# Attention and FP4 feed-forward block: job order within a unit, a lead of 23 chunks, and value products two units behind their scores

## The chip, the cores and the metric

The kernel runs on one core of a Trainium2 chip. The metric is the device time of one execution in microseconds (us). The kernel before was run three times: 900.21, 903.68 and 904.95 us, median 903.68. A further execution was profiled; the trace rows below come from it.

## What is computed

The input x is 4 x 1024 tokens of width 128. It is normalized, and two branches are added to it:

```python
xn = _layernorm(x, axis=-1)
x = x + attn(xn, Wq, bq, Wk, bk, Wv, bv, Wo, bo) + ffn(xn, w_gate, w_up, w_down)
# attn: 16 heads of 8 columns
scores = jnp.einsum('bhqd,bhkd->bhqk', q, k) * scale + bias[None]   # alibi bias
attn = jax.nn.softmax(scores, axis=-1)
ctx = jnp.einsum('bhqk,bhkd->bhqd', attn, v)
# ffn: every operand of the three products is rounded to FP4 in blocks of 16
h = jax.nn.silu(fp4_linear(x, w_gate)) * fp4_linear(x, w_up)        # 352 columns
return fp4_linear(h, w_down)
```

## The kernel before, in words

Softmax needs the maximum of each row of scores. The kernel computes every score twice. In the first pass TensorE makes a **chunk**: 128 queries of one head against all 1024 keys, as two matmuls of 512 columns into one of two PSUM slots `mx` (`half_chunk`, L925 to L938). VectorE reduces the chunk to its negated maximum (L811). The maxima of 16 chunks (four heads, half of the queries) are split into two bf16 parts (L816, L817), transposed (`turn`, L944), copied by ScalarE (L636), and sent through DRAM into two rows of the operand `q_op` (`max_rows`, L379 and L382). In the second pass a score matmul therefore already has its maximum subtracted; it gives 128 keys x 512 queries of one head (`score`, L947 to L956), and ScalarE takes the exponential (L630) into `probs`. A value product (`value_product`, L958 to L969) multiplies the `probs` of four heads with v, as four matmuls beside each other in the columns of the array, in two passes, and accumulates over eight key tiles in the PSUM bank `pv`.

The work is cut in 256 **units** U: four heads, half of the queries, one key tile of 128. A unit holds four scores (j = 0 to 3), the value product of the unit before, and two chunks (i = 0, 1) of the first pass, which runs LEAD = 22 chunks ahead. Every eighth unit closes a `pv` bank: ScalarE copies it (L667), then the job `pvT` transposes and scales it. Score banks are a ring of three in `low`; a matmul into the ring waits until the entry three places before is emptied, and all entries of the ring are emptied by ScalarE. The two slots `mx` are a ring of their own, emptied by VectorE.

The order in TensorE's queue is written out by hand (L1067 to L1078). For i = 0, 1 and kh = 0, 1 it is half a chunk, then score j = 2i + kh. The jobs of the unit (`extras(U)`) come after i = 0, and value product U - 1 comes at the end. Which rows of the array an operand uses depends on its head: `head_rows(x, ...)` gives rows 0 up for x = 0 and rows 64 up for x = 1. A chunk has 51 rows, a score 53. These two lines set x:

```python
    x, g, qt = c % 2, c // 8, c // 2 % 4          # in chunk(pos); c = pos % 16, pos = LEAD + 2 * U + i
HEAD = ((1, 0), (1, 1), (0, 0), (0, 1))           # (x, g) of score j
```

Jobs, with the offset f of a unit in a feed-forward period of 15 units (16 periods, for 256 tokens each): `xT` 0, `gate` 1 and 2, `up` 4, `hT` 12 and 13, `down` 14; the quantization of the next period is spread over GpSimd and VectorE (`block_maxima` L784, `block_scales` L795 to L798, `powers` L804) between f = 5 and 12. For token groups 2 to 7 there are `xnT`, `q`, `k`, `v`, and at the end of a batch `ctxT` and `wo`. `up`, `down`, `pvT`, `wo` and `bvo` use an `mx` slot and are emptied by VectorE; the others use a bank of `low` and are emptied by ScalarE.

Of the kernel before, what the change touches and what calls it, by code (L numbers as in the profile page):

```python
# [23 lines left out]
KT = S // P  # L24
HALF = S // 2
UNITS = 2 * KT
NU = B * QUADS * UNITS
# [41 lines left out]

LEAD = 22
CHUNKS = 2 * B * QUADS * UNITS
HALVES = 2 * B * QUADS

# [1 line left out]
def ffn_unit(p):  # L77
    return 10 + 15 * p


def group_unit(g):
    return 13 + 60 * (g // 2 - 1) + 15 * (g % 2)


def turn_unit(m):
# [18 lines left out]
def extras(U):  # L104

    out = []
    p, f = divmod(U - ffn_unit(0), ffn_unit(1) - ffn_unit(0))
    if 0 <= p < NP:
        out += {0: [("xT", p)], 1: [("gate", p, 0)], 2: [("gate", p, 1)], 4: [("up", p)], 12: [("hT", p, 0)],
                13: [("hT", p, 1)], 14: [("down", p)]}.get(f, [])  # L110
    for g in range(2, NG):
        if 0 <= U - group_unit(g) < 4:
            out.append((("xnT", "q", "k", "v")[U - group_unit(g)], g))
    out += [("turn", m) for m in range(LEAD // 16, HALVES) if turn_unit(m) == U]
    m, f = U // KT - 1, U % KT
    if m >= 0:
        out += [("pvT", m)] * (f == 2)
        if m // 2 % QUADS == QUADS - 1:
            out += {4: [("ctxT", m // 8 * 2 + m % 2)], 5: [("wo", m // 8 * 2 + m % 2)]}.get(f, [])
    out += {0: [("bvo",)], 7: [("gT",)], 8: [("uT",)], 9: [("dT",)]}.get(U, [])  # L120
    return out


IN_DVE_RING = ("up", "down", "pvT", "wo", "bvo")


def rings():

    act, dve = {}, {}

    def to_act(*key):
        act[key] = len(act)

    def to_dve(*key):
        dve[key] = len(dve)

    for g in range(2):
        for name in ("xnT", "q", "k", "v"):
            to_act(name, g)
    for pos in range(LEAD):  # L140
        to_dve("max", pos)
        if pos == 17:
            to_act("turn", 0)
    for U in range(NU + KT):
        for i in range(2):
            if LEAD + 2 * U + i < CHUNKS:
                to_dve("max", LEAD + 2 * U + i)
            for j in (2 * i, 2 * i + 1):
                if U < NU:
                    to_act("exp", U, j)  # L150
            for job in extras(U) if i == 0 else ():
                (to_dve if job[0] in IN_DVE_RING else to_act)(*job)
    return act, dve


# [3 lines left out]
def attn_ffn(nc, x, wq, bq, wk, bk, wv, bv, wo, bo, wg, wu, wd, out):  # L159
    with ExitStack() as ctx:  # L160
# [260 lines left out]
        def _(pool):  # L421
# [136 lines left out]
            for U in range(NU):  # L558
                b, u = divmod(U, QUADS * UNITS)
                if u == 2:  # L560
                    add_bias(b)
                for g in range(2, NG):
                    if U == group_unit(g) - 2:
                        normalize(g)
                    if U == group_unit(g) + 2:
                        three_parts(g, 0, "q")
                    if U == group_unit(g) + 3:
                        three_parts(g, 1, "k")
                for p in range(NP):
                    if U == ffn_unit(p) + 3:  # L570
                        swish(p)
                    if U == ffn_unit(p) + 5:
                        scale_to_grid(p + 1)
                    if U == ffn_unit(p) + 7:
                        round_on_grid(p + 1)


# [1 line left out]
        def _(act):  # L579
# [77 lines left out]
            for U in range(NU + KT):  # L657
                if 3 <= U < NU:
                    act.wait_ge(pv_done, U - 2)
                for j in range(2):  # L660
                    exponential(U, j)
                if U % KT == 1 and U > KT:
                    m = U // KT - 1
                    act.wait_ge(pv_done, U - 1)
                    if m:
                        act.wait_ge(mx_full, MX["pvT", m - 1] + 1)
                    nc.scalar.copy(pv_s[:], pv).then_inc(pv_kept, 1)  # L667
                for job in extras(U):
                    kind, p = job[0], job[1] if len(job) > 1 else 0
                    if kind == "xT":  # L670
                        full("xT", p)
                        if p:
                            act.wait_ge(mx_full, MX["up", p - 1] + 1)
                        nc.scalar.copy(xqT[:], bank("xT", p)[:, 0:PW]).then_inc(st_free, 1)
                    elif kind == "gate":
                        t = job[2]
                        full("gate", p, t)
                        if p:
                            act.wait_ge(mx_free, MX["up", p - 1] + 1)
                        nc.scalar.activation(tanh_s[:, t * I:(t + 1) * I], bank("gate", p, t)[:, 0:I], ACT.Tanh, scale=0.5)  # L680
                        nc.scalar.copy(gate_s[:, t * I:(t + 1) * I], bank("gate", p, t)[:, 0:I]).then_inc(st_free, 1)  # L681
                    elif kind == "hT":
                        t = job[2]
                        full("hT", p, t)
                        if p:
                            act.wait_ge(mx_full, MX["down", p - 1] + 1)
                        nc.scalar.copy(hqT[t][:], bank("hT", p, t)[:, 0:3 * P]).then_inc(st_free, 1)
                    elif kind == "xnT":
                        keep_xnT(p)
                    elif kind == "q":  # L690
                        keep_q(p)
                    elif kind == "k":
                        keep_k(p)
                    elif kind == "v":
                        keep_v(p)
                    elif kind == "turn":
                        keep_turn(p)
                    elif kind == "ctxT":
                        full("ctxT", p)
                        if p:  # L700
                            act.wait_ge(mx_full, MX["wo", p - 1] + 1)
                        nc.scalar.copy(ctxT_s[:], bank("ctxT", p)).then_inc(st_free, 1)
                    elif kind in ("gT", "uT"):
                        full(kind)
                        nc.scalar.copy((gT_s if kind == "gT" else uT_s)[:], bank(kind)[:, 0:I]).then_inc(st_free, 1)
                    elif kind == "dT":
                        full("dT")
                        nc.scalar.copy(dT_s[:, 0:2 * P], bank("dT")[:, 0:2 * P])
                        nc.scalar.copy(dT_s[0:96, 2 * P:3 * P], bank("dT")[0:96, 2 * P:3 * P]).then_inc(st_free, 1)
                for j in range(2, 4):  # L710
                    exponential(U, j)


        @block.vector
        def _(dve):
# [74 lines left out]
            def block_scales(job):  # L790
                n = job_cols(job) // BLK
                settle()
                if job:
                    dve.wait_ge(quant_ok, job)
                mark(nc.vector.tensor_scalar(sc[:, 0:n], am[:, 0:n], 1.0 / 6.0, 1e-12, ALU.mult, ALU.max))  # L795
                link(nc.vector.tensor_scalar(scn[:, 0:n], am[:, 0:n], (1.0 + 2.0 ** -22) / 6.0, 1e-12,
                                             ALU.mult, ALU.max))
                link(nc.vector.reciprocal(inv[:, 0:n], scn[:, 0:n]))  # L798
                dve.sem_inc(inv_ok, 1)  # L799

            def powers(job):
                w = job_cols(job)
# [67 lines left out]
            norm_scale(1)  # L870
            block_maxima(0)
            block_scales(0)
            for pos in range(LEAD):
                if pos == 8:
                    powers(0)
                reduce_chunk(pos)

            for U in range(NU + KT):
                for i in range(2):
                    pos = LEAD + 2 * U + i  # L880
                    if i == 1:
                        for job in extras(U):
                            job_on_vector(job)
                    if pos < CHUNKS:
                        reduce_chunk(pos)
                    for p in range(NP):
                        if U == ffn_unit(p) + 5 and i == 0:
                            block_maxima(p + 1)
                        if U == ffn_unit(p) + 5 and i == 1:
                            block_scales(p + 1)  # L890
                        if U == ffn_unit(p) + 7 and i == 0:
                            powers(p + 1)


# [1 line left out]
        def _(pe):  # L896
# [170 lines left out]
            for U in range(NU + KT):  # L1067
                for i in range(2):
                    pos = LEAD + 2 * U + i
                    for kh in range(2):  # L1070
                        if pos < CHUNKS:
                            half_chunk(pos, kh)
                        if U < NU:
                            score(U, 2 * i + kh)
                    for job in extras(U) if i == 0 else ():
                        job_on_array(job)
                if 0 < U <= NU:
                    value_product(U - 1)  # L1078


# [24 lines left out]
```

## Time and profile before

| | |
|---|---|
| median of three runs | 903.68 us (900.21 to 904.95) |
| profiled execution | 894.07 us |
| its span, first to last instruction | 892.3 us |
| TensorE matmul busy | 772.9 us (87%) |
| VectorE busy | 741.1 us (83%) |
| ScalarE busy | 633.0 us (71%) |
| GpSimd busy | 349.3 us (39%) |
| mean granted TensorE clock | 0.962 |

The page gives busy time per engine; that of TensorE contains modelled matmul ends, so two matmuls whose starts lie 0.22 us apart are each shown as 0.39 us long. Starts are exact, and lengths of units are read from starts.

### The profile page before, as it was taken

The numbers are of one execution on the slowest core, as the hardware profiler recorded it, in microseconds if no ns is written. First come the engines' busy times: TensorE is split into PE (matmuls) and PEld (weight loads), VectorE is DVE, ScalarE is ACT, GpSimd is POOL, SyncE is SP. The second block draws the span as 40 slices with busy tenths as digits, with TensorE's granted clock in tenths as the row PEclk, the third lists the DMA queues.
The fourth block names the chain that finished last, engine by engine and source line by source line (L and its number), as shares of the span: only waits on it lengthen the run. The fifth ranks groups of instructions, "written<-read, shape, count | busy, mean of one in ns | idle before, by whom it ended". The sixth has DMA issues, their size and how long they took to land.

```text
span 892.3 us, 13552 instructions
## 1 busy us (share of the span) xinstructions
PE 772.9 (87%) x4939; PEld 225.7 (25%) x4939; DVE 741.1 (83%) x878; ACT 633.0 (71%) x1262; POOL 349.3 (39%) x271
## 2 busy tenths in 40 slices
PE   3279989898989989897989989898989898979896
PEld 2012223221223323231323323222213231313222
DVE  7898898889888888978898888989897989898920
ACT  4106878777777878776877778777777687767775
POOL 7272172624226373715053553615152505141320
PEclk9557999999999999999999999999999999999999
DMA  5900020131001020320102020310102000000000
GB/s 156 256 13 2 1 72 3 52 92 36 3 13 37 13 72 2 101 44 1 37 2 49 13 73 1 107 37 1 37 2 49 13 3 1 2 1 2 2 1 24
DMA packets 32826, 31.83 MB, mean 36 GB/s; under 512 B 4344, under 2 KB 26552, under 8 KB 32760
## 3 DMA queue, kind: packets, MB, share of 16 engines
q1 hardware_dynamic: 32760, 30.96, 12.8%
q8 instruction: 40, 0.66, 0.3%
q14 instruction: 26, 0.21, 0.1%
HBM read 15.91 MB, written 15.04 MB: 35 GB/s over the span
## 4 chain that ended last, share of the span: by engine, by line
PE 58%; DVE 27%; ACT 8%; issue 4%; POOL 2%; DMA 1%; SPq 0%; ACTq 0%; DVEq 0%; POOLq 0%
PE low L966 22%; DVE neg_max L811 19%; PE mx L936 18%; ACT probs L630 6%; PE low L955 5%; PE mx L1005 3%; PE mx L989 3%; PE low L983 2%; DVE am L784 1%; DVE mb L804 1%; PE low L922 1%; ACT pv_s L667 1%; PE low L997 1%; DVE hid L826 1%; DVE inv L798 1%
## 5 line engine op out<-in xcount | busy, mean ns | idle before, releaser
L811 DVE TENSOR_REDUCE neg_max<-mx 128x1 f32<-128x1024 f32 x512 | 611.6, 1221 | 91.6 <-PE mx L936 80.2
L630 ACT ACTIVATE probs<-low 128x512 f32<-128x512 f32 x1024 | 552.0, 603 | 182.1 <-PE low L955 180.4
L936 PE MATMUL mx<-k_op,q_op 51*128 51x512 bf16 x1024 | 318.5, 398 | 55.9 <-DVE neg_max L811 33.4
L955 PE MATMUL low<-q_op,k_op 53*128 53x512 bf16 x1024 | 329.0, 389 | 8.0 <-ACT probs L630 2.5
L966 PE MATMUL low<-probs,v_op 128*32 128x512 f32 x2048 | 277.4, 614 | 7.1 <-ACT pv_s L667 5.9
L551 POOL TENSOR_SCALAR tanh_s<-tanh_s 128x704 f32<-128x704 f32 x16 | 31.7, 1982 | 313.7 <-ACT gate_s L681 313.7
L936 PEld LDWEIGHTS mx<-k_op,q_op 51*128 51x128 bf16 x1024 | 62.6, 95 | 358.5 <-DVE neg_max L811 197.2
L955 PEld LDWEIGHTS low<-q_op,k_op 53*128 53x128 bf16 x1024 | 68.5, 94 | 76.5 <-ACT probs L630 63.8
L489 POOL TENSOR_SCALAR mb<-mb 128x960 f32<-128x960 f32 (+2 forms) x17 | 58.8, 3456 | 39.6 <-DVE mb L804 37.9
L966 PEld LDWEIGHTS low<-probs,v_op 128*32 128x32 f32 x2048 | 40.5, 108 | 89.9 <-issue 46.1
L477 POOL TENSOR_TENSOR zb<-hid,inv 128x704 f32<-128x704 f32 x16 | 22.2, 1387 | 97.7 <-DVEq L799 97.7
L491 POOL TENSOR_TENSOR zb<-zb,mb 128x960 f32<-128x960 f32 (+2 forms) x17 | 38.2, 2247 | 1.3
L490 POOL TENSOR_TENSOR zb<-zb,mb 128x960 f32<-128x960 f32 (+2 forms) x17 | 38.2, 2244 | 1.4
L636 ACT COPY max_t<-low 32x128 bf16<-32x128 bf16 x32 | 8.1, 254 | 39.1 <-PE low L944 39.0
L983 PE MATMUL low<-gT_s,xqT 128*128 128x352 f32 x64 | 27.5, 511 | 0.2
L552 POOL TENSOR_TENSOR gate_s<-tanh_s,gate_s 128x704 f32<-128x704 f32 x16 | 27.0, 1686 | 1.3
L944 PE MATMUL low<-ident_b,neg_parts 128*32 128x128 bf16 x32 | 7.2, 224 | 22.4 <-DVE neg_parts L817 19.4
L1005 PE MATMUL mx<-dT_s,hqT 128*128 128x128 f32 (+1 forms) x192 | 25.7, 283 | 0.0
L1016 PE MATMUL mx<-ident,pv_s 128*128 128x128 f32 x128 | 20.2, 280 | 5.0 <-DVE neg_max L811 3.9
L1005 PEld LDWEIGHTS mx<-dT_s,hqT 128*128 128x128 f32 (+1 forms) x192 | 22.6, 191 | 6.8 <-DVE neg_max L811 4.7
L989 PE MATMUL mx<-uT_s,xqT 128*128 128x352 f32 x64 | 23.2, 485 | 0.0
L501 POOL TENSOR_TENSOR hq<-zb,sc 128x704 f32<-128x704 f32 x16 | 22.3, 1392 | 1.3
(120 smaller groups left out, 522.3 us busy)
## 6 DMA issues: line engine op xcount, KB each, us to landing
q_op<-q_rows SPq DMA_DIRECT2D x32, 192.0 KB, 3.8
k_op<-k_rows SPq DMA_DIRECT2D x32, 192.0 KB, 4.7
q_rows<-qp SPq DMA_DIRECT2D x8, 384.0 KB, 2.6
k_rows<-kp SPq DMA_DIRECT2D x8, 384.0 KB, 3.2
x_s<-in_L_attn_inputs_dram SPq DMA_DIRECT2D x8, 256.0 KB, 3.7
q_rows<-qp SPq DMA_DIRECT2D x8, 256.0 KB, 3.1
k_rows<-kp SPq DMA_DIRECT2D x8, 256.0 KB, 3.1
out_dram<-o_s SPq DMA_DIRECT2D x8, 256.0 KB, 2.3
```

The costliest lines, as they stand in the source:

```text
L489: link(nc.gpsimd.tensor_scalar(m, m, 1.0, ROUND, ALU.max, ALU.mult))
L490: link(nc.gpsimd.tensor_tensor(z, z, m, ALU.add))
L491: link(nc.gpsimd.tensor_tensor(z, z, m, ALU.subtract))
L551: link(nc.gpsimd.tensor_scalar(tanh_s[:], tanh_s[:], 1.0, None, ALU.add))
L630: nc.scalar.activation(probs[U % 3][:, 2 * g + x, :], bank("exp", U, j), ACT.Exp).then_inc(st_free, 1)
L811: nc.vector.tensor_reduce(to, slot("max", pos)[:], AX.X, ALU.max, negate=True).then_inc(mx_free, 1)
L936: ins = nc.tensor.matmul(slot("max", pos)[:, 512 * kh:512 * kh + 512], q, k, start=True, stop=True)
L955: nc.tensor.matmul(bank("exp", U, j), k_op[quad][r, g, kt * P:(kt + 1) * P], q_op[quad][r, g, half * HALF:(half + 1) * HALF], start=True, ...
L966: ins = nc.tensor.matmul(pv[32 * hh:32 * hh + 32, :], v_op[b % 2][:, kt, 4 * quad + hh, :], probs[U % 3][:, hh, :], start=(kt == 0), stop= ...
L983: nc.tensor.matmul(bank("gate", p, t)[:, 0:I], xqT[:, t * P:(t + 1) * P], gT_s[:], start=True, stop=True).then_inc(st_full, 1)
L989: ins = nc.tensor.matmul(slot("up", p)[:, 512 * t:512 * t + I], xqT[:, t * P:(t + 1) * P], uT_s[:], start=True, stop=True)
L1005: ins = nc.tensor.matmul(slot("down", p)[:, t * P:(t + 1) * P], hqT[t][0:n, c * P:(c + 1) * P], dT_s[0:n, c * P:(c + 1) * P], start=(c == ...
```

## The change

LEAD goes from 22 to 23. Jobs are split in two lists: `middle(U)` holds those that VectorE empties and stays after i = 0; `end(U)` holds those that ScalarE empties and goes behind the last score, in TensorE's queue and in ScalarE's. The value product made in unit U is that of U - 2, and it comes after i = 0 ahead of the middle jobs where there are any, otherwise after i = 1. ScalarE copies a finished `pv` one unit later (after the first exponential), and `pvT` moves from f = 2 to f = 3 of its eight units. `up` moves from offset 4 to 5. The jobs of token groups move: `xnT`, `q`, `k`, `v` stood at 13 to 16 (plus the period), now at 19, 20, 21 and 28. VectorE's maxima, scales, inverses and powers, and GpSimd's scaling and rounding, move by about a unit, and the inverses become a step of their own behind the second chunk.

```diff
-LEAD = 22
+LEAD = 23
 def group_unit(g):
-    return 13 + 60 * (g // 2 - 1) + 15 * (g % 2)
+    return 19 + 60 * (g // 2 - 1) + 15 * (g % 2)
...
-        out += {0: [("xT", p)], 1: [("gate", p, 0)], 2: [("gate", p, 1)], 4: [("up", p)], 12: [("hT", p, 0)],
+        out += {0: [("xT", p)], 1: [("gate", p, 0)], 2: [("gate", p, 1)], 5: [("up", p)], 12: [("hT", p, 0)],
                 13: [("hT", p, 1)], 14: [("down", p)]}.get(f, [])
-        if 0 <= U - group_unit(g) < 4:
-            out.append((("xnT", "q", "k", "v")[U - group_unit(g)], g))
+        out += {0: [("xnT", g)], 1: [("q", g)], 2: [("k", g)], 9: [("v", g)]}.get(U - group_unit(g), [])
-        out += [("pvT", m)] * (f == 2)
+        out += [("pvT", m)] * (f == 3)
...
+def middle(U):
+    return [job for job in extras(U) if job[0] in IN_DVE_RING]
+def end(U):
+    return [job for job in extras(U) if job[0] not in IN_DVE_RING]
...
 # GpSimd
-                    if U == group_unit(g) + 2:
+                    if U == group_unit(g) + 4:
                         three_parts(g, 0, "q")
-                    if U == group_unit(g) + 3:
+                    if U == group_unit(g) + 4:
                         three_parts(g, 1, "k")
-                    if U == ffn_unit(p) + 5:
+                    if U == ffn_unit(p) + 6:
                         scale_to_grid(p + 1)
-                    if U == ffn_unit(p) + 7:
+                    if U == ffn_unit(p) + 8:
                         round_on_grid(p + 1)
...
 # ScalarE
-                for j in range(2):
+                for j in range(4):
                     exponential(U, j)
-                if U % KT == 1 and U > KT:
-                    act.wait_ge(pv_done, U - 1)
-                    nc.scalar.copy(pv_s[:], pv).then_inc(pv_kept, 1)
-                for job in extras(U):
+                    if j == 0 and U % KT == 2 and U > KT:
+                        act.wait_ge(pv_done, U - 2)
+                        nc.scalar.copy(pv_s[:], pv).then_inc(pv_kept, 1)
+                for job in end(U):
...
-                for j in range(2, 4):
-                    exponential(U, j)
...
 # VectorE
-                        if U == ffn_unit(p) + 5 and i == 0:
+                        if U == ffn_unit(p) + 5 and i == 1:
                             block_maxima(p + 1)
-                        if U == ffn_unit(p) + 5 and i == 1:
-                            block_scales(p + 1)
-                        if U == ffn_unit(p) + 7 and i == 0:
+                        if U == ffn_unit(p) + 6:
+                            (block_scales if i == 0 else block_inverses)(p + 1)
+                        if U == ffn_unit(p) + 8 and i == 0:
                             powers(p + 1)
...
 # TensorE
-                    for job in extras(U) if i == 0 else ():
+                    if 2 <= U < NU + 2 and i == (0 if middle(U) else 1):
+                        value_product(U - 2)
+                    for job in middle(U) if i == 0 else ():
                         job_on_array(job)
-                if 0 < U <= NU:
-                    value_product(U - 1)
+                for job in end(U):
+                    job_on_array(job)
```

## Rows read from the trace of the kernel before

**Rows 1.** Stretches: length; busy PE, PEld, DVE, ACT, POOL; granted clock; DMA share, GB/s.
```profile
66.70:880.40 813.70, 735.40 (x4827) 214.03 (x4827) 683.42 (x750) 615.81 (x1229) 310.13 (x224) 0.98 0.10 27
66.70:77.60 10.90, 10.01 (x42) 2.17 (x41) 8.30 (x8) 6.30 (x12) 4.75 (x8) 0.50 0.01 2
...
408.70:412.10 3.40, 3.40 (x18) 0.54 (x15) 1.47 (x2) 1.26 (x3) 0.48 (x1) 0.50 0.00 0
```

**Rows 2.** Timeline of a unit without jobs (start, length, engine, line), then the next unit's start.
```profile
424.18 0.09 PEld L955 LDWEIGHTS low<-q_op,k_op 53*128 53x128 bf16 x1
424.18 0.39 PE L936 MATMUL mx<-k_op,q_op 51*128 51x512 bf16 x1
424.18 0.39 PE L955 MATMUL low<-q_op,k_op 53*128 53x512 bf16 x1
...
424.41 0.38 PE L936 MATMUL mx<-k_op,q_op 51*128 51x512 bf16 x1
...
424.67 2.07 ACT L630 ACTIVATE probs<-low 128x512 f32<-128x512 f32 x4 [0.39 <-PE low L955]
...
425.32 0.39 PE L955 MATMUL low<-q_op,k_op 53*128 53x512 bf16 x1
...
425.64 1.07 PE L966 MATMUL low<-probs,v_op 128*32 128x512 f32 x8
...
426.64 0.39 PE L936 MATMUL mx<-k_op,q_op 51*128 51x512 bf16 x1
```

**Rows 3.** Timeline behind the last chunk: scores j = 0, 1, 2 alone.
```profile
869.37 0.60 PE L955 MATMUL low<-q_op,k_op 53*128 53x512 bf16 x3
```

**Rows 4.** Timeline of a unit with a gate job, then the next unit's start.
```profile
392.97 0.39 PE L936 MATMUL mx<-k_op,q_op 51*128 51x512 bf16 x1
...
393.51 0.86 PE L983 MATMUL low<-gT_s,xqT 128*128 128x352 f32 x2
...
394.30 0.39 PE L936 MATMUL mx<-k_op,q_op 51*128 51x512 bf16 x1
...
394.44 0.47 ACT L680 ACTIVATE tanh_s<-low 128x352 f32<-128x352 f32 x1
...
394.78 0.47 ACT L681 COPY gate_s<-low 128x352 f32<-128x352 f32 x1
...
395.92 0.39 PE L936 MATMUL mx<-k_op,q_op 51*128 51x512 bf16 x1
```

**Rows 5.** TensorE's stretches for `down` and `up` in the chain of waits.
```profile
383.38 1.53 PE mx L1005 x12
...
399.26 1.40 PE mx L989 x4
```

**Rows 6.** VectorE's work beside the chunks: `up` and maxima.
```profile
400.68 0.89 DVE L826 SCALAR_TENSOR_TENSOR hid<-gate_s,mx 128x704 f32<-128x704 f32 x1 [0.16 <-PE mx L989]
...
403.98 0.88 DVE L784 TENSOR_REDUCE am<-hid 128x44 f32<-128x704 f32 x1
```

**Rows 7.** Timeline of one `pvT` job on TensorE and VectorE.
```profile
867.25 0.66 PE L1016 MATMUL mx<-ident,pv_s 128*128 128x128 f32 x4
...
867.94 0.26 DVE L841 RECIPROCAL pv_r<-mx 128x16 f32<-128x16 f32 x1 [2.23 <-PE mx L1016]
```

**Rows 8.** Timeline: first chunk matmuls of units 40 and 55.
```profile
193.51 0.39 PE L936 MATMUL mx<-k_op,q_op 51*128 51x512 bf16 x1
...
240.21 0.39 PE L936 MATMUL mx<-k_op,q_op 51*128 51x512 bf16 x1
```

**Rows 9.** Timeline: three of VectorE's chunks back to back.
```profile
413.98 3.48 DVE L811 TENSOR_REDUCE neg_max<-mx 128x1 f32<-128x1024 f32 x3
```

**Rows 10.** Waits: who waited for whom (us in total, times, longest).
```profile
PE low L944 <- DVE neg_parts L817: 19.4, 13, 2.7
...
PEld low L966 <- ACT pv_s L667: 16.4, 28, 0.9
```

**Rows 11.** The tile `m_rows`: how long its DMAs take to land.
```profile
DMA to landing us min/median/max: 1.3/1.3/4.6
```

More of the change, by code:

```diff
@@ L150, in rings @@
                     to_act("exp", U, j)
-            for job in extras(U) if i == 0 else ():
-                (to_dve if job[0] in IN_DVE_RING else to_act)(*job)
+            for job in middle(U) if i == 0 else ():
+                to_dve(*job)
+        for job in end(U):
+            to_act(*job)
     return act, dve
@@ L659, in _ @@
                     act.wait_ge(pv_done, U - 2)
-                for j in range(2):
+                for j in range(4):
                     exponential(U, j)
-                if U % KT == 1 and U > KT:
-                    m = U // KT - 1
-                    act.wait_ge(pv_done, U - 1)
-                    if m:
-                        act.wait_ge(mx_full, MX["pvT", m - 1] + 1)
-                    nc.scalar.copy(pv_s[:], pv).then_inc(pv_kept, 1)
-                for job in extras(U):
+                    if j == 0 and U % KT == 2 and U > KT:
+                        m = U // KT - 1
+                        act.wait_ge(pv_done, U - 2)
+                        if m:
+                            act.wait_ge(mx_full, MX["pvT", m - 1] + 1)
+                        nc.scalar.copy(pv_s[:], pv).then_inc(pv_kept, 1)
+                for job in end(U):
                     kind, p = job[0], job[1] if len(job) > 1 else 0
@@ L795, in block_scales, with block_inverses @@
                 mark(nc.vector.tensor_scalar(sc[:, 0:n], am[:, 0:n], 1.0 / 6.0, 1e-12, ALU.mult, ALU.max))
-                link(nc.vector.tensor_scalar(scn[:, 0:n], am[:, 0:n], (1.0 + 2.0 ** -22) / 6.0, 1e-12,
+                mark(nc.vector.tensor_scalar(scn[:, 0:n], am[:, 0:n], (1.0 + 2.0 ** -22) / 6.0, 1e-12,
                                              ALU.mult, ALU.max))
-                link(nc.vector.reciprocal(inv[:, 0:n], scn[:, 0:n]))
-                dve.sem_inc(inv_ok, 1)
+            def block_inverses(job):
+                n = job_cols(job) // BLK
+                settle()
+                nc.vector.reciprocal(inv[:, 0:n], scn[:, 0:n]).then_inc(inv_ok, 1)
             def powers(job):
@@ L872, in _ @@
             block_scales(0)
+            block_inverses(0)
             for pos in range(LEAD):
@@ L880, in _ @@
                     pos = LEAD + 2 * U + i
-                    if i == 1:
-                        for job in extras(U):
-                            job_on_vector(job)
+                    for job in middle(U) if i == 1 else ():
+                        job_on_vector(job)
                     if pos < CHUNKS:
@@ L1074, in _ @@
                             score(U, 2 * i + kh)
-                    for job in extras(U) if i == 0 else ():
+                    if 2 <= U < NU + 2 and i == (0 if middle(U) else 1):
+                        value_product(U - 2)
+                    for job in middle(U) if i == 0 else ():
                         job_on_array(job)
-                if 0 < U <= NU:
-                    value_product(U - 1)
+                for job in end(U):
+                    job_on_array(job)
 _INS = ["L0_attn_inputs", "L0_attn_Wq", "L0_attn_bq", "L0_attn_Wk", "L0_attn_bk", "L0_attn_Wv", "L0_attn_bv",
```

## The prediction

> **What bounds the kernel now.** I read the stretches first, then one unit in the timeline, then the chain of waits. The main loop takes 813.7 us of the span [rows 1]: VectorE is busy 683 of them (84%), TensorE by its modelled ends 735. Neither is full, so the loop is bound by how the two, and ScalarE, hand over to each other, unit by unit.
>
> A unit without jobs takes 426.64 - 424.18 = 2.46 us [rows 2]. Two limits meet there. VectorE needs two chunks of 1.13 to 1.22 us (three back to back take 3.48 [rows 9], so 1.13 from start to start). And there is a loop over three banks: score 0 starts at 0.00, its exponential at 0.49, takes 0.60, score 3 may follow it at 1.14, the value product at 1.46, and the next unit at 2.46 [rows 2]. Unit 40 to unit 55, one feed-forward period with two `pvT` and two `turn`, takes 46.70 us [rows 8]: 15 x 2.46 = 36.9, the rest is jobs and waits.
>
> The line to look at is the first pair of [rows 2]. The half chunk (L936) and score 0 (L955) start together at 424.18, and the next half chunk comes 0.22 us later, so two matmuls of 512 columns cost the time of one. They can, because the chunk uses rows 0 up of the array (x = 0, pos even) and score 0 rows 64 up (x = 1). [Rows 3] have both cases: scores 0 and 1 share rows, score 2 does not, and the three last 0.60 us together. One is shown as 0.39, so the second costs 0.21 and the third nothing.
>
> **The change, part by part.** **LEAD 23.** pos = 23 + 2U + i is odd for i = 0, so its chunk has x = 1; HEAD is not touched, so scores 0 and 1 have x = 1 too. For i = 1 both have x = 0. Every half chunk now shares its rows with the score behind it. In a unit without jobs the order is then hc, s0, hc, s1 on rows 64 up, and hc, s2, hc, s3 on rows 0 up; only the third half chunk can lie beside s1. That is seven steps of 0.22 where there were four, 0.66 us more of TensorE. In the loop of the banks score 0 starts at 0.22 and not at 0.00, all else follows: 0.22 + 0.49 + 0.60 + 0.05 + 0.32 + 1.00 = 2.68 us. TensorE's own work gives 6 x 0.22 to s3, + 0.32 + 1.00 = 2.64, so both limits lie there. Over the 245 units that have chunks, +0.22 x 245 = **+54 us**. One chunk more ahead of the loop: +1.2 us.
>
> The Trainium skill ("TensorE: Matmul & The Clock Gate", Part 2, back-to-back issue gap) has 131 ns per matmul of 512 columns in a stream of weight loads and matmuls. The 0.21 us of [rows 3] speaks against it here; by it the +54 would be 0.13 x 245 = 32.
>
> **ScalarE's jobs at the end.** Before, a gate unit took 395.92 - 392.97 = 2.95 us, so the 0.79 us of the gate on TensorE [rows 4] cost 0.49: it stood in the slack ahead of s2 and s3. Behind the value product there is no slack, it costs 0.79, and tanh and copy (0.47 each [rows 4]) end about 0.35 after the next exponential could begin. That is 1.14 for 0.49, and 32 x 0.65 = **+21**. `xT` and `hT` are short on both engines and cost about what they did: -2. The jobs of the six token groups lose their slack too: about +6.
>
> **Middle jobs behind a value product.** VectorE has reduced chunk 0 at 2.03, and the job's matmul is full only at 1.97 + its length. `up` is 1.40 long, `down` 1.53 [rows 5], `pvT` 0.55 ([rows 7], less the modelled end). VectorE idles 1.4 us in `up` and has 0.89 for it and 0.88 for the larger part of the maxima [rows 6], beside scales, inverses and powers. I walked through units 40 to 54 with these durations, each matmul behind its slot or bank. Lengths: 3.05, 3.46, 4.18, 3.31, 3.28, 4.50 (`up`), 3.47, 3.48, 3.05, 2.95, 2.98, 3.30, 3.74, 3.31, 4.18 (`down`), and 0.7 of wait behind `down`: 52.9 us against 46.7 of [rows 8], +6.2. In classes over the loop: `up` with what follows +10, `down` +14, `pvT` +6, `wo` and `ctxT` +8.
>
> **What it gives back.** The maxima are complete at i = 0, and `turn` asks for them a unit and a half later, so TensorE's 19.4 us of waiting on neg_parts [rows 10] go; with the 0.55 that VectorE's split still costs, -15. The copy of `pv` is asked for later in its unit (16.4 us now [rows 10]): -3. Four dips of the clock as in [rows 1] (3.4 us at 0.50, the 1.2 GHz level), each behind a stretch in which TensorE waited, cost at most 1.7 each; a busier TensorE should lose them: -7. The loop's first 10.9 us run at 0.50 [rows 1], where the serial steps cost double: +5.
>
> **Sum.** 54 + 21 - 2 + 6 + 10 + 14 + 6 + 8 - 15 - 3 - 7 + 5 + 1 = +98. The walked period gives nearly the same: 6.2/15 x 245 = 101, with the last three terms 100. Both charge every wait in full, though one that falls behind another is absorbed. Done in the same way for before, 2.46 x 255 and the jobs come to 860, where the loop takes 814; of the 233 above the plain units 80% were real. With 0.8 on the +44 that jobs bring, +89. I take **+91**: profiled 894.07 + 91 = 985. The median of runs stood 9.6 above the profiled execution, so **994 us** as a median, +10%.
>
> **Costs at nothing.** The first `max_rows` chain has two units and more between `turn` and the score that needs it; it is a matmul, a copy, two issues and two landings of 1.3 us [rows 11], some 4.5 us of 6. If a landing takes the 4.6 of [rows 11], score 0 is late by 1 to 2. Gathers and rows of parts move together with their groups and stay ten units ahead. GpSimd's rounding starts a unit later and `hT` half a unit later; before, it ended 3 us ahead, and units are longer now. ScalarE's wait for `pv_done` is covered by score 0, which stands behind that value product.
>
> **Rivals.** (a) *The order gains more than I charge* (12%): nearly every wait of VectorE is absorbed. The bound is TensorE's own work, 2.68 x 245 + 25 for the tail + 152 of jobs + 25 of gate, copy and start = 860 against 814: +46 to +60, 950 to 965. (The 152 are 25 for gates, 21 for `xT` and `hT`, 22 for `up`, 24 for `down`, 18 for `pvT` and 42 for groups and smaller ones.) For it: maxima, scales and inverses are spread over more chunks. Against it: `up` and `down` leave VectorE idle for 1.4 us right ahead of them.
> (b) *Rows do not matter*, or the waits saved outweigh them: **faster** (6%). If a half chunk and a score of the same rows still started together, the unit stayed at 2.46. Then -15 - 3 - 7 against +6 to +30 of the middle jobs and gates, the best case some 885 and the worst about no change (2 of the 6). It decides at the spacing of L936 and L955: below 0.1 us it is right. [Rows 3] speak against it.
> (c) *The third half chunk does not slip beside s1* (6%): s3 at 1.54, a unit of 2.86, another +0.18 x 245 = +44: 1038.
> (d) *Weights of the same rows are not loaded ahead* (2%): each serial step would cost 0.22 + 0.09 of load (the weight load in [rows 2]), for six steps in 245 units +132, so about 1125. The second score of [rows 3] loads its own weights and costs 0.21, which is against it. The Trainium skill (same page, Part 3, the mechanism) says that weight loads overlap matmuls in flight only where the row groups differ; by this rule (d) would be the forecast, and the trace does not agree.
> (e) *The maxima land late* (3%): 32 times 1 to 2 us on top, 1025 to 1060.
> The forecast itself has 71%, its own range 965 to 1025: the lower end absorbs half of what the jobs bring and loses all dips, the upper is the sum in full (+101) with +20 for collisions of groups, `wo` and `pvT` in one unit.
>
> **Numbers.** The range is 952 to 1030: the forecast's with most of (a) and the nearer part of (e); (b), (d) and most of (c) stay out. A measurement of this kernel tells about 0.5%, some 4.5 us. Faster 4% and within 0.5% 2% are the two parts of (b); slower 94% is all the rest.
>
> **What would show it.** In the changed kernel's timeline: L936 and L955 in a unit without jobs 0.22 apart, not at one time; 2.68 us from unit to unit; a gate unit near 3.5 with the next one longer; no wait of L944 on neg_parts; VectorE idle for about 1.4 us ahead of L826; fewer or no dips of the clock behind the start. Pairs that still start together, or plain units of 2.46, make the prediction wrong in its main step; plain units of 2.68 with a total under 950 make it wrong in the jobs.

## The result and the profile after

The changed kernel takes 996.05 us (median of four runs, 994.02 to 1004.77) against 902.14 us (900.21 to 904.95): a ratio of 1.106, 95% interval 1.098 to 1.113. A fourth execution of the kernel before, 900.60 us, brings its median from 903.68 to 902.14. The change makes it slower by 10.6%, where 994 us, slower, was forecast. The profiled execution took 994.02 us, with a span of 992.1 us at a mean clock of 0.954. In the ratios below, executions of the kernel before that took 914 to 919 us at a lower granted clock are left out.

The page after, the lines of the engines (PE is TensorE's matmuls, PEld its weight loads) and of the costliest groups (busy us, mean ns, then idle time ahead of them and who ended it):

```profile
PE 907.5 (91%) x4939; PEld 292.7 (30%) x4939; DVE 733.5 (74%) x878; ACT 636.8 (64%) x1262; POOL 347.0 (35%) x271
...
L823 DVE TENSOR_REDUCE neg_max<-mx 128x1 f32<-128x1024 f32 x512 | 608.2, 1219 | 152.4 <-PE mx L948 149.4
L641 ACT ACTIVATE probs<-low 128x512 f32<-128x512 f32 x1024 | 543.3, 603 | 223.2 <-PE low L967 216.3
```

Nothing was added and the long instructions kept their lengths. VectorE and ScalarE are busy for nearly the same time as before, which is a smaller share of a longer span; both wait more for TensorE, VectorE 149.4 us for chunks where it was 80.2. TensorE's busy time grew from 772.9 to 907.5 us with the same 4939 matmuls: they no longer lie beside each other.

A unit without jobs after, in the timeline, beside [rows 2]:

```profile
243.98 0.39 PE L948 MATMUL mx<-k_op,q_op 51*128 51x512 bf16 x1
243.99 0.10 PEld L967 LDWEIGHTS low<-q_op,k_op 53*128 53x128 bf16 x1
...
244.21 0.38 PE L967 MATMUL low<-q_op,k_op 53*128 53x512 bf16 x1
...
244.43 0.38 PE L948 MATMUL mx<-k_op,q_op 51*128 51x512 bf16 x1
...
244.64 0.38 PE L967 MATMUL low<-q_op,k_op 53*128 53x512 bf16 x1
...
244.65 0.39 PE L948 MATMUL mx<-k_op,q_op 51*128 51x512 bf16 x1
...
244.68 2.06 ACT L641 ACTIVATE probs<-low 128x512 f32<-128x512 f32 x4 [0.94 <-PE low L967]
...
244.88 0.38 PE L967 MATMUL low<-q_op,k_op 53*128 53x512 bf16 x1
...
245.09 0.38 PE L948 MATMUL mx<-k_op,q_op 51*128 51x512 bf16 x1
...
245.33 0.39 PE L967 MATMUL low<-q_op,k_op 53*128 53x512 bf16 x1
...
245.65 1.06 PE L978 MATMUL low<-probs,v_op 128*32 128x512 f32 x8
...
246.65 0.39 PE L948 MATMUL mx<-k_op,q_op 51*128 51x512 bf16 x1
```

Read the starts. Half chunk and score are 0.22 us apart where they started together. Only the third half chunk, at 244.65, lies beside the score at 244.64, since it is the first on the other rows. The next unit begins at 246.65, so the unit is 2.67 us long, for 2.46 before and 2.68 forecast.

A unit with `up` shows the second cost, VectorE's wait behind a value product that stands ahead of the job:

```profile
233.63 1.07 PE L978 MATMUL low<-probs,v_op 128*32 128x512 f32 x8
...
234.63 1.45 PE L1001 MATMUL mx<-uT_s,xqT 128*128 128x352 f32 x4
...
236.01 0.39 PE L948 MATMUL mx<-k_op,q_op 51*128 51x512 bf16 x1
...
236.12 0.89 DVE L838 SCALAR_TENSOR_TENSOR hid<-gate_s,mx 128x704 f32<-128x704 f32 x1 [1.35 <-PE mx L1001]
```

The waits, in total (engine, tile and line that waited, who was waited for, us, times, longest):

```profile
DVE x_s L846 <- PE mx L1017: 36.7, 16, 12.9
...
DVE pv_r L853 <- PE mx L1028: 23.8, 20, 8.3
...
DVE hid L838 <- PE mx L1001: 22.0, 16, 2.2
...
PEld low L978 <- ACT pv_s L678: 14.5, 28, 1.3
...
PE low L956 <- DVE neg_parts L829: 1.2, 1, 1.2
```

For `up` it is 22.0 us in 16 times, 1.4 each, as forecast. Before, the first three, ahead of VectorE's work for `down`, `pvT` and `up`, were 17.0, 11.9 and 2.9 us.

### The profile page after: what moved, and what is told of

Its sections match the earlier page's. It is cut to its first block, busy times and chain, and to the rows that moved or that the text cites. A ratio compares the mean times of both kernels' runs of the same rounds, so it can differ in the third digit from the quotient of the medians.

```text
span 992.1 us, 13535 instructions
## 1 busy us (share of the span) xinstructions
PE 907.5 (91%) x4939; PEld 292.7 (30%) x4939; DVE 733.5 (74%) x878; ACT 636.8 (64%) x1262; POOL 347.0 (35%) x271
## 4 chain that ended last, share of the span: by engine, by line
PE 72%; DVE 18%; ACT 5%; issue 3%; SPq 1%; DMA 1%; ACTq 0%; DVEq 0%
PE low L978 24%; PE mx L948 17%; PE low L967 16%; DVE neg_max L823 11%; ACT probs L641 3%; PE low L995 3%; PE mx L1017 2%; PE mx L1001 2%; PE low L1009 2%; ACT pv_s L678 1%; PE mx L1028 1%; DVE hid L838 1%; PE low L934 1%; DVE am L793 1%; PE mx L1041 1%
## 5 line engine op out<-in xcount | busy, mean ns | idle before, releaser
L823 DVE TENSOR_REDUCE neg_max<-mx 128x1 f32<-128x1024 f32 x512 | 608.2, 1219 | 152.4 <-PE mx L948 149.4
L641 ACT ACTIVATE probs<-low 128x512 f32<-128x512 f32 x1024 | 543.3, 603 | 223.2 <-PE low L967 216.3
L948 PE MATMUL mx<-k_op,q_op 51*128 51x512 bf16 x1024 | 358.6, 401 | 47.8 <-DVE neg_max L823 25.6
L967 PE MATMUL low<-q_op,k_op 53*128 53x512 bf16 x1024 | 358.9, 388 | 11.0 <-ACT probs L641 8.1
L978 PE MATMUL low<-probs,v_op 128*32 128x512 f32 x2048 | 280.8, 622 | 4.9 <-ACT pv_s L678 3.1
L948 PEld LDWEIGHTS mx<-k_op,q_op 51*128 51x128 bf16 x1024 | 92.2, 96 | 278.2 <-DVE neg_max L823 157.5
L967 PEld LDWEIGHTS low<-q_op,k_op 53*128 53x128 bf16 x1024 | 95.1, 95 | 145.4 <-ACT probs L641 86.0
L846 DVE TENSOR_TENSOR x_s<-mx,x_s 128x256 f32<-128x256 f32 x16 | 6.8, 424 | 36.7 <-PE mx L1017 36.7
L838 DVE SCALAR_TENSOR_TENSOR hid<-gate_s,mx 128x704 f32<-128x704 f32 x16 | 14.2, 888 | 22.0 <-PE mx L1001 22.0
L691 ACT ACTIVATE tanh_s<-low 128x352 f32<-128x352 f32 x32 | 14.9, 464 | 21.9 <-PE low L995 21.3
L853 DVE RECIPROCAL pv_r<-mx 128x16 f32<-128x16 f32 x32 | 8.2, 257 | 24.5 <-PE mx L1028 23.8
```

Of the source, the lines that this page charges most:

```text
L641: nc.scalar.activation(probs[U % 3][:, 2 * g + x, :], bank("exp", U, j), ACT.Exp).then_inc(st_free, 1)
L823: nc.vector.tensor_reduce(to, slot("max", pos)[:], AX.X, ALU.max, negate=True).then_inc(mx_free, 1)
L948: ins = nc.tensor.matmul(slot("max", pos)[:, 512 * kh:512 * kh + 512], q, k, start=True, stop=True)
L967: nc.tensor.matmul(bank("exp", U, j), k_op[quad][r, g, kt * P:(kt + 1) * P], q_op[quad][r, g, half * HALF:(half + 1) * HALF], start=True, ...
L978: ins = nc.tensor.matmul(pv[32 * hh:32 * hh + 32, :], v_op[b % 2][:, kt, 4 * quad + hh, :], probs[U % 3][:, hh, :], start=(kt == 0), stop= ...
```

## The experiments

Two theories stood against each other. *Rows*: a half chunk and a score that use the same rows of the array run one after the other. *Order*: the loss comes from the places of the jobs and of the value product. Times are medians; ratios are against runs of the kernel before on the same chip.

**Rows made complementary again, in the changed kernel.** Complementary means that a half chunk and the score behind it use different rows.

```diff
-HEAD = ((1, 0), (1, 1), (0, 0), (0, 1))
+HEAD = ((0, 0), (0, 1), (1, 0), (1, 1))
```

> The changed kernel with HEAD = ((0,0),(0,1),(1,0),(1,1)), so that with LEAD 23 each half chunk again uses other rows than the score behind it. Theory 'rows' (half chunk and score of the same rows run one after the other, +0.22 us per unit in 245 units, and the slow first 10 us of the loop): half chunk and score start together, a unit without jobs takes 2.46 us, and the time falls from 996 to between 910 and 935 us. Rival 'order' (the loss comes from the place of the jobs and of the value product): the time stays within 10 us of 996.

Measured: 918.68 us, ratio 1.021 (1.017 to 1.024). In its timeline the pairs start together again, and the most frequent length of a unit is 2.46 us:

```profile
224.75 0.39 PE L948 MATMUL mx<-k_op,q_op 51*128 51x512 bf16 x1 [0.44 <-DVE neg_max L823]
224.75 0.39 PE L967 MATMUL low<-q_op,k_op 53*128 53x512 bf16 x1
...
224.98 0.38 PE L948 MATMUL mx<-k_op,q_op 51*128 51x512 bf16 x1
224.98 0.38 PE L967 MATMUL low<-q_op,k_op 53*128 53x512 bf16 x1
```

So of the 10.6% loss, 2.1% belong to the order and 8.5%, some 77 us, to the rows. What the granted clock did with the rows is contained in the 77: the profiled execution here has 6.8 us of the low clock inside the loop, the changed kernel 27.3.

**The same by the other way: LEAD 22 in the changed kernel**, HEAD as it was.

```diff
-LEAD = 23
+LEAD = 22
```

> The changed kernel with LEAD 22 and HEAD as it was: the same complementary rows as by swapped heads, reached the other way. Theory 'rows': 914 to 924 us, as the run with swapped heads (918.7). Rival (it was the order of heads in the scores or in probs, not the rows, that the swap changed): it stays above 960.

Measured: 920.06 us, ratio 1.025 (1.023 to 1.027). Either edit alone removes 8 of the 10.6%; what both change is whether chunk and score share rows.

**Rows alone, in the kernel before**: LEAD stays 22, in the old order.

```diff
-HEAD = ((1, 0), (1, 1), (0, 0), (0, 1))
+HEAD = ((0, 0), (0, 1), (1, 0), (1, 1))
```

> The kernel before with HEAD = ((0,0),(0,1),(1,0),(1,1)) and nothing else: LEAD stays 22, so each half chunk now shares its rows with the score behind it, in the old order of jobs. Theory 'rows': a unit without jobs goes from 2.46 to 2.68 us, and the time from 902 to between 950 and 975 us, since jobs that stood in TensorE's slack are no longer free. Rival 'order': within 5 us of 902.

Measured: 1012.63 us, ratio 1.127 (1.121 to 1.132), more than the 975 expected. The rows cost 112 us here and 77 us in the new order. A gate unit shows the larger part of why:

```profile
217.21 0.39 PE L936 MATMUL mx<-k_op,q_op 51*128 51x512 bf16 x1
...
217.43 0.38 PE L955 MATMUL low<-q_op,k_op 53*128 53x512 bf16 x1
...
217.65 0.38 PE L936 MATMUL mx<-k_op,q_op 51*128 51x512 bf16 x1
...
217.87 0.38 PE L955 MATMUL low<-q_op,k_op 53*128 53x512 bf16 x1
...
218.18 0.86 PE L983 MATMUL low<-gT_s,xqT 128*128 128x352 f32 x2
...
218.97 0.39 PE L936 MATMUL mx<-k_op,q_op 51*128 51x512 bf16 x1
...
219.94 1.06 PE L966 MATMUL low<-probs,v_op 128*32 128x512 f32 x8
...
220.94 0.39 PE L936 MATMUL mx<-k_op,q_op 51*128 51x512 bf16 x1
```

The gate stands between score 1 and the third half chunk, so these cannot lie beside each other: all eight steps are serial. The unit is 220.94 - 217.21 = 3.73 us long, against 2.95 in [rows 4]: 0.78 for the rows where a plain unit pays 0.21. Against the trace of the kernel before, and away from stretches of low clock, the 156 units with a job are 0.58 us longer on the mean and the 70 without one 0.18. In the new order most jobs stand at the end and leave score 1 and the third half chunk together.

**The lead alone**, in the kernel before, with HEAD going along so that the rows stay complementary.

```diff
-LEAD = 22
+LEAD = 23
-HEAD = ((1, 0), (1, 1), (0, 0), (0, 1))
+HEAD = ((0, 0), (0, 1), (1, 0), (1, 1))
```

> The kernel before with LEAD = 23 and HEAD swapped along with it: the lead alone, with the rows as complementary as before. Theory 'rows': 902 plus or minus 4 us; the maxima are complete half a unit earlier, so the 19.4 us that the transpose of the maxima waits for VectorE's split mostly go, but only a part of them shows. Rival (a lead of 23 costs something of its own): over 910 us.

Measured: 898.12 us, ratio 0.996 (0.993 to 0.999). TensorE's wait for neg_parts fell from 19.4 to 2.1 us, and the time by some 4 us: a fifth of the wait. The lead is not the only way to end it: with LEAD 22 and `turn` at the unit's end it is 1.2 us in the changed kernel and 2.7 in the kernel before (the next run).

**ScalarE's jobs at the unit's end, alone**, in the kernel before.

The lists `middle` and `end` are those of the changed kernel, and ScalarE's order goes along (both left out here).

```diff
...
-            for job in extras(U) if i == 0 else ():
-                (to_dve if job[0] in IN_DVE_RING else to_act)(*job)
+            for job in middle(U) if i == 0 else ():
+                to_dve(*job)
+        for job in end(U):
+            to_act(*job)
...
-                    for job in extras(U) if i == 0 else ():
+                    for job in middle(U) if i == 0 else ():
                         job_on_array(job)
                 if 0 < U <= NU:
                     value_product(U - 1)
+                for job in end(U):
+                    job_on_array(job)
```

> The kernel before with the jobs that ScalarE empties moved to the unit's end (behind the last score and the value product, and behind the fourth exponential), and nothing else: LEAD 22, rows complementary, value product one unit behind. Theory (the jobs lose TensorE's slack, gate units cost 1.14 us over a plain one where they cost 0.49): +10 to +25 us, 912 to 927. Rival (the new place of these jobs is a gain, paid for only by the rows): 902 or below.

Measured: 927.12 us, ratio 1.030 (1.027 to 1.033). A gate unit in its timeline, behind a value product:

```profile
251.97 0.39 PE L946 MATMUL mx<-k_op,q_op 51*128 51x512 bf16 x1
...
253.43 1.06 PE L976 MATMUL low<-probs,v_op 128*32 128x512 f32 x8
...
254.43 0.86 PE L993 MATMUL low<-gT_s,xqT 128*128 128x352 f32 x2
...
255.22 0.39 PE L946 MATMUL mx<-k_op,q_op 51*128 51x512 bf16 x1
...
255.32 0.46 ACT L692 ACTIVATE tanh_s<-low 128x352 f32<-128x352 f32 x1 [0.79 <-PE low L993]
```

The unit is 3.25 us long on TensorE, a plain one with the 0.79 of the gate, and tanh begins only when the next unit's score 0 has already been issued. The time lies at the upper end of what was expected.

**Gates taken out of the end jobs**: as above, with the 32 gate jobs back behind i = 0.

```diff
-    return [job for job in extras(U) if job[0] in IN_DVE_RING]
+    return [job for job in extras(U) if job[0] in IN_DVE_RING + ("gate",)]
...
-    return [job for job in extras(U) if job[0] not in IN_DVE_RING]
+    return [job for job in extras(U) if job[0] not in IN_DVE_RING + ("gate",)]
...
```

> The kernel before with ScalarE's jobs at the unit's end (927.1), but the 32 gate jobs back behind i = 0 and the second exponential. By the prediction's term the gates are 21 of the loss: 902 to 909 us. Rival (all end jobs cost alike, through lost slack): 915 to 922.

Measured: 902.63 us, ratio 1.004 (1.001 to 1.007). The gates are 24 of the 27 us.

**The value product's new place, alone**, in the kernel before, with `pvT` and the copy of `pv` one unit later.

```diff
...
+                    middle = [job for job in extras(U) if job[0] in IN_DVE_RING]
+                    if 2 <= U < NU + 2 and i == (0 if middle else 1):
+                        value_product(U - 2)
                     for job in extras(U) if i == 0 else ():
                         job_on_array(job)
-                if 0 < U <= NU:
-                    value_product(U - 1)
```

> The kernel before with the value product made two units behind its scores, ahead of the middle jobs where there are any and behind i = 1 otherwise (with the copy of pv and pvT one unit later); all jobs stay after i = 0, LEAD 22, rows complementary. The step of the prediction (VectorE idles about 1 us more ahead of each middle job, 73 units, against 16 us of waits for the copy of pv): 900 to 915 us. Rival, from the 919 of the changed kernel with complementary rows against 927 for the end jobs alone: the new place of the value product gives back some 8 us, so 885 to 898.

Measured: 921.97 us, ratio 1.025 (1.017 to 1.033): the rival, that it gives back some 8 us, was wrong, and the bound of 915 was too low. The profiled execution of this run also has 44.4 us of low clock inside the loop, against 13.6 in the kernel before; what part of the loss that makes is not shown.

**Only the due times**: the changed kernel with complementary rows, all jobs in the middle and the value product at the end again. HEAD, ScalarE's order, the copy of `pv` and `pvT` go along (left out here).

```diff
...
-                    if 2 <= U < NU + 2 and i == (0 if middle(U) else 1):
-                        value_product(U - 2)
-                    for job in middle(U) if i == 0 else ():
+                    for job in extras(U) if i == 0 else ():
                         job_on_array(job)
-                for job in end(U):
-                    job_on_array(job)
+                if 0 < U <= NU:
+                    value_product(U - 1)
```

> The changed kernel with complementary rows (HEAD swapped), all jobs after i = 0 again and the value product one unit behind at the unit's end again: what is left of the change is LEAD 23, up at offset 5, the later token groups and the maxima, scales and inverses spread over more chunks. Theory (these are gains, since VectorE's work between offsets 5 and 8 held TensorE up for some 3 us per period): 880 to 898 us. Rival (it only moves the waits): within 4 us of 898.

Measured: 894.82 us, ratio 0.996 (0.993 to 0.999). That fits both expectations. It is level with the lead alone (0.996 each), so the new due times gave nothing that these runs resolve. It also has a new wait:

```profile
PE low L1009 <- POOLq L520: 12.2, 11, 2.1
```

It was 0.9 us before. GpSimd begins its rounding a unit later, so TensorE waits for it at `hT`, unless that job also moves to the unit's end.

**Due times and the value product's place**, jobs in the middle, rows complementary; HEAD and ScalarE's order go along.

```diff
...
                     if 2 <= U < NU + 2 and i == (0 if middle(U) else 1):
                         value_product(U - 2)
-                    for job in middle(U) if i == 0 else ():
+                    for job in extras(U) if i == 0 else ():
                         job_on_array(job)
-                for job in end(U):
-                    job_on_array(job)
```

> As the run with the due times only, but with the value product two units behind, placed as in the changed kernel. Only the end jobs are undone, beside the rows. If the end jobs are what costs (27 us alone): 885 to 900 us; it lies above the run with the due times only if the value product ahead of the middle jobs costs, below it if it gains.

Measured: 923.84 us, ratio 1.029 (1.026 to 1.033), outside the 885 to 900 expected: with the end jobs undone the loss stayed, so in the changed kernel they are not what costs. It lies 29 us above the run with the due times only, so the value product's new place or its distance does.

**The same with every value product behind i = 1.**

```diff
-                    if 2 <= U < NU + 2 and i == (0 if middle(U) else 1):
+                    if 2 <= U < NU + 2 and i == 1:
```

> As the run with due times and value products (923.8), but every value product, still two units behind its scores, stands behind i = 1, never ahead of a middle job. If that place is what costs (VectorE idles while the value product and then the job's matmuls run): back to 889 to 899 us, and VectorE's idle time ahead of L826 and of the job down falls to that of the kernel before. Rival (being two units behind costs, through the later copy of pv): it stays at 915 or more.

Measured: 899.05 us, ratio 1.002 (0.999 to 1.004). Two units of distance, with the later copy of `pv`, cost 0.6% (ratios 0.996 and 1.002), some 5 us; the place ahead of middle jobs costs 25 us. The waits of VectorE show it, in the run before this one and in this one:

```profile
DVE x_s L846 <- PE mx L1017: 36.1, 16, 15.6
...
DVE hid L838 <- PE mx L1001: 18.7, 16, 2.2
```
```profile
DVE x_s L846 <- PE mx L1017: 16.5, 14, 12.4
...
DVE hid L838 <- PE mx L1001: 3.2, 14, 0.4
```

**The fourth corner: end jobs, value products behind i = 1**, in the changed kernel with HEAD swapped.

```diff
-HEAD = ((1, 0), (1, 1), (0, 0), (0, 1))
+HEAD = ((0, 0), (0, 1), (1, 0), (1, 1))
...
-                    if 2 <= U < NU + 2 and i == (0 if middle(U) else 1):
+                    if 2 <= U < NU + 2 and i == 1:
```

> The changed kernel with complementary rows (HEAD swapped) and every value product, two units behind, behind i = 1; ScalarE's jobs stay at the unit's end. It is the fourth corner beside jobs in the middle and value products at the end (899), jobs in the middle and value products ahead of middle jobs (924), and end jobs with value products ahead (919). If the two costs add up, the end jobs alone give 899 + 919 - 924 = 894. If each alone costs and together they overlap: 920 to 930, near the 927 of the end jobs put into the kernel before.

Measured: 912.62 us, ratio 1.015 (1.010 to 1.021), between both expectations. With complementary rows and the new due times the four corners are:

| | value product behind i = 1 | ahead of middle jobs |
|---|---|---|
| ScalarE's jobs in the middle | 1.002 | 1.029 |
| ScalarE's jobs at the end | 1.015 | 1.021 |

Each move costs by itself, 1.3 and 2.7%, and both together 1.9% over the first corner. With the value product ahead of the middle jobs, moving ScalarE's jobs to the end is thus a gain of 0.8%. The difference in the lower row, 0.6%, is within the intervals of its two runs. A part of this is plain: with the jobs in the middle TensorE waits 13 to 14 us for GpSimd at `hT` in both runs, which the end jobs avoid (0.4 us and none). That favours the lower row and says nothing on why the value product's place costs 2.7% in one row and at most little in the other; this stays open.

**The changed kernel profiled again**, with no edit.

> The changed kernel unaltered, profiled once more, for the stretches at the 1.2 GHz clock. If the clock belongs to the order of the work: again some 27 us of dips inside the loop at about the same places and 17 us at its start. If it is chance: other places, and a total anywhere from 7 to 30 us; the time within 8 us of 996 either way.

Measured: 1000.77 us, one run. Inside the loop it has 47.8 us of dips, where 27.3 would have been a repetition and 30 was the most expected of chance, and 17.4 at its start. The six dips of the first execution are there again at the same places, and three more: neither expectation describes it. See the last section.

## Why the prediction was right

- **Rows.** The mechanism and its size in a plain unit were right: 0.22 us between starts, the third half chunk beside score 1, 2.67 us per unit. The term was undersized as a whole: 54 for the units and 5 for the slow start, 59 in all, against 77. The 54 charge the plain unit's 0.22 to every unit. The profiled executions of the changed kernel and of the one with complementary rows, taken unit by unit, show what is missing. Away from low clock, the 60 units with a middle job are 0.46 us longer, since the job parts score 1 from the third half chunk, and the other 163 are 0.19 longer: 59 us in all. The 20 units that one of the two ran at the low clock give 13.5 us more, and 3 lie ahead of the loop.
- **Jobs at the end.** Forecast +21 for the gates, +25 for all of them; put into the kernel before, the runs give 24 and 27. In the changed kernel they are not a cost: beside the value product's new place they gain 0.8%, as the four corners show.
- **Value product ahead of middle jobs.** `up` +10, `down` +14, `pvT` +6, `wo` and `ctxT` +8 are 38, 30 with the factor 0.8. Measured 25 with jobs in the middle, but 6 with jobs at the end, the order that the changed kernel has. VectorE's 1.4 us ahead of `up` came as walked through.
- **The sum of the order was oversized.** Everything beside the 59 of the rows was forecast at +32 and measured at +19. The two costs came near alone and did not add up. No run shows why they come to 19 together; the factor 0.8 for absorbed waits was too mild.
- **What it gives back.** The wait on neg_parts went (1.2 us in one time are left), but the lead gave 4 us and not the 15 I booked. A wait that ends is worth what the next limit leaves, here a fifth. Nor was the lead needed for it.
- **The clock** was wrong in sign. I booked -7 for dips that a busier TensorE would lose. They went from 13.6 to 27.3 us.
- **The walked period** came out to the number. Units 40 to 55, forecast 52.9 us, took 52.93:

```profile
214.16 0.53 PE L948 MATMUL mx<-k_op,q_op 51*128 51x512 bf16 x2
...
267.09 0.53 PE L948 MATMUL mx<-k_op,q_op 51*128 51x512 bf16 x2
```

  Each row holds the last half chunk of a unit with `down` and the first of the next unit, which follows it within 0.14 us since it uses the other rows; the rows are 52.93 us apart. That is luck in part: unit 43 took 4.62 us for 3.31, since it has a `v` projection after the change that I left out, and units 42, 44 and 48 together took 1.4 us less than walked. Unit 45 with its `up` took 4.48 for 4.50.
- **The total** of 994 against 996 rests on errors that cancel: rows 18 too small, order 13 too large. A second luck lies in the step from a profiled execution to the median. The forecast for the profiled one was 985, +91, and it took 994.02, +100; of the 9.6 us put on top for the median only 2.0 were there after the change.
- **Rivals.** Absorption alone (a) falls, though the order did absorb more than I charged. Rows without effect (b) fall by the two edits that restore them. The third half chunk does lie beside score 1, against (c). Weights of the same rows load ahead, against (d): the load of score 0 starts at 243.99, while the half chunk of 243.98 on the same rows is in flight, and the serial steps are 0.22 apart with their loads in them. So the rule of the Trainium skill, in "TensorE: Matmul & The Clock Gate", Part 3, that weight loads overlap matmuls in flight only where the row groups differ, does not describe this stream. No score waits for late maxima, against (e).

## What to carry to other kernels

When one matmul is cheap only because it lies beside another in different rows of the array, the order of the two streams is part of the kernel: here a lead changed by one flipped a parity and cost 8.5%, without an instruction added. Look for pairs of starts within a few nanoseconds in the trace before and ask of each edit whether it keeps them. A job put into an engine's slack costs less than its length (a gate 0.49 us of its 0.79 before); put at the unit's end it cost all of it. Moves of this kind did not add up here, so price them together.

## What the runs showed of the hardware

The granted clock fell more often although TensorE was busy for more of the time. Stretches of the changed kernel (length; busy PE, PEld, DVE, ACT, POOL; clock), each dip behind the 3.4 us ahead of it:

```profile
180.60:184.00 3.40, 3.06 (x13) 0.90 (x12) 3.06 (x4) 2.42 (x5) 0.00 (x0) 1.00 0.01 2
184.00:187.40 3.40, 3.40 (x15) 0.86 (x15) 3.07 (x6) 1.15 (x3) 0.25 (x1) 0.50 0.00 0
...
402.50:405.90 3.40, 2.40 (x12) 0.90 (x12) 3.14 (x8) 2.09 (x5) 0.21 (x1) 1.00 0.02 5
405.90:412.70 6.80, 6.80 (x28) 1.39 (x27) 5.73 (x7) 3.34 (x6) 4.50 (x7) 0.50 0.00 1
```

and of the kernel before:

```profile
405.30:408.70 3.40, 1.37 (x10) 0.56 (x12) 3.18 (x7) 1.09 (x2) 1.49 (x2) 1.00 0.00 0
```

Before, TensorE had been busy 1.4 to 1.7 of the 3.4 us ahead of each of the four dips, when the clock went to 1.2 GHz. After, it had been busy 2.4 to 3.4 of them ahead of the six, by the page's measure, and it fell all the same. What ran in the two stretches shown were half chunks and scores one at a time on half of the rows, with no value product. So a busy TensorE was no safeguard. What decides stays open. With the rows made complementary the changed kernel has 6.8 us of dips, and rows shared in the old order have 30.7; but the two kernels with complementary rows that have all jobs in the middle and the value product ahead of `up`, `down` and `pvT` have 44.4 and 30.7 as well. Each is one profiled execution.

In the two executions of the changed kernel the first six dips start at the same places within 0.3 us. The sixth lasts longer in the second execution, and three more follow:

```profile
183.80:187.20 3.40, 3.40 (x15) 0.90 (x15) 3.12 (x6) 1.11 (x3) 0.20 (x1) 0.50 0.00 0
...
733.40:740.20 6.80, 6.80 (x31) 1.62 (x24) 4.89 (x7) 2.78 (x6) 1.96 (x2) 0.50 0.02 4
...
846.00:852.80 6.80, 6.80 (x29) 1.48 (x28) 5.63 (x7) 3.37 (x7) 2.75 (x3) 0.50 0.00 0
```

By the records of the granted clock the dips inside the loop are 27.3 us in the first execution and 47.8 in the second, and the loop to the last unit is 908.6 and 915.7 us long. The 7.1 us for 20.5 us of dips make 0.35 us lost per microsecond at 1.2 GHz, and 6.9 of them lie in units that one of the two ran at the low clock. That it is less than a half is probably because VectorE sets part of the time; no run shows this. The kernel before has 13.6 us of dips and 10.9 us of slow start, the changed one 27.3 and 17.4; at 0.35 these 20 us more are, as an estimate, about 7 us of the 100 between the two profiled executions.
